# Unread products in the four message passes of a graph and expert network, and another split of the PSUM banks

## The reference, cut to what matters

```
def _gine(x, src, dst, edge_attr, W1, b1, W2, b2, eW, eb, eps):
    e = edge_attr @ eW + eb                                # 31875 x 32 @ 32 x 256
    m = jax.nn.relu(x[src] + e)                            # a gather of 31875 rows of 256
    agg = jax.ops.segment_sum(m, dst, num_segments=N)      # the message pass
    h = (1.0 + eps) * x + agg
    return jax.nn.relu(h @ W1 + b1) @ W2 + b2
h = _gine(x, ...)                                          # pass 1 of 4
for k in range(1, 4):
    y = relu(layernorm(h, gamma[k], beta[k]))
    h = h + _gine(y, ...)                                  # passes 2 to 4
```

## Time and profile before

| | us |
|---|---|
| median of 3 runs | 4527.91 |
| the profiled execution | 4526.65 |
| its span | 4525.0 |
| first to last line 957 in pass 1 | 145 to 549 |
| in pass 2 | 632 to 1023 |
| in pass 3 | 1105 to 1496 |
| in pass 4 | 1576 to 1968 |

### The profile page before, as it was taken

One profiled execution on the slowest core, in us unless ns is written; L12 is line 12 of the kernel. 1 busy time (PEld: TensorE's weight loads), 2 busy tenths in 40 slices (PEclk: granted clock), 3 DMA queues, 4 the chain that ended last, 5 costly groups with the idle time before them and its releaser, 6 DMA issues. The chain is left out here.

```text
span 4525.0 us, 52039 instructions
## 1 busy us (share of the span) xinstructions
PE 2865.0 (63%) x16062; PEld 2374.0 (52%) x16063; DVE 2207.9 (49%) x4940; ACT 726.2 (16%) x1635; POOL 1870.5 (41%) x1982
## 2 busy tenths in 40 slices
PE   3566657775777667750568256767769639947492
PEld 2456545563565455540557123336758639936391
DVE  7566645554555545566246556771254421144213
ACT  1122112221222212210112000002210113300120
POOL 4566456664666366636315666711100020020212
PEclk8788877877777777875769566667979869968696
DMA  5733223332333233313423133317756459945693
GB/s 129 287 87 88 68 67 90 90 84 59 88 89 90 53 90 89 90 34 130 161 54 109 41 92 93 94 43 254 245 185 234 157 183 327 309 149 171 210 338 119
DMA packets 358089, 607.55 MB, mean 134 GB/s; under 512 B 82185, under 2 KB 240187, under 8 KB 355131
## 3 DMA queue, kind: packets, MB, share of 16 engines
q1 hardware_dynamic: 245816, 357.76, 24.3%
q0 software_dynamic: 88640, 214.25, 17.0%
q10 hardware_dynamic: 23363, 32.26, 2.0%
HBM read 508.28 MB, written 95.81 MB: 134 GB/s over the span
## 5 line engine op out<-in xcount | busy, mean ns | idle before, releaser
L831 POOL DMA_INDIRECT gine_got<-gine_table,src x1056 | 1017.4, 963 | 561.2 <-issue 271.4
L905 PE MATMUL gine_p_sum<-gine_hot,gine_got 128*128 128x128 f32 x4224 | 782.9, 330 | 204.5 <-issue 174.0
L905 PEld LDWEIGHTS gine_p_sum<-gine_hot,gine_got 128*128 128x128 f32 x4224 | 690.2, 240 | 289.8 <-issue 266.0
L957 DVE TENSOR_TENSOR gine_got<-gine_got,gine_p_edge 128x512 f32<-128x512 f32 x528 | 360.5, 683 | 601.5 <-DMA unpack_rows<-in_edge_rows 250.7
L916 ACT ACTIVATE gine_got<-gine_got 128x512 f32<-128x512 f32 x528 | 332.2, 630 | 1309.5 <-DVE gine_got L957 946.9
L940 DVE TENSOR_TENSOR stack_acc<-stack_acc,gine_p_sum 128x256 f32 x1056 | 437.6, 414 | 43.0 <-issue 1.5
L489 POOL DMA_INDIRECT adjacency<-value,place x264 | 280.3, 1062 | 390.3 <-POOLq L54 191.4
L892 PE MATMUL gine_p_edge<-gine_w_a,edge_space 128*128 128x256 bf16 x1056 | 329.1, 326 | 98.7 <-issue 94.1
L893 PE MATMUL gine_p_edge<-gine_w_b,edge_space 128*128 128x256 bf16 x1056 | 328.7, 325 | 98.9 <-issue 85.8
L1416 PE MATMUL ffn_p_h<-ffn_xt,ffn_w 128*128 128x128 f32 x2864 | 347.7, 280 | 1.7 <-DVE ffn_xt L1468 0.5
L1416 PEld LDWEIGHTS ffn_p_h<-ffn_xt,ffn_w 128*128 128x128 f32 x2864 | 337.5, 196 | 4.6 <-issue 2.5
(11 more groups left out here) (399 smaller groups left out, 3365.4 us busy)
## 6 DMA issues: line engine op xcount, KB each, us to landing
gcn_a<-adjacency SPq DMA_DIRECT2D x270, 320.0 KB
ffn_w<-in_L_ffn_W SPq DMA_DIRECT2D x74, 1024.0 KB
ffn_w<-in_L_ffn_w SPq DMA_DIRECT2D x60, 1024.0 KB
ffn_w<-in_L_ffn_w SPq DMA_DIRECT2D x90, 512.0 KB
adjacency<-zero_row ACTq DMA_DIRECT2D x3, 7200.0 KB
gine_got<-gine_table,src POOLq DMA_INDIRECT x1056
h_table<-score_rows SPq DMA_DIRECT2D x15, 1056.0 KB
edge_space<-dst_lines ACTq DMA_DIRECT2D x3, 2816.0 KB
```

The lines of the kernel that those rows point to most:

```text
L831: pool.indirect_dma_start(got[:, c % RING, :], None, table, bass.IndirectOffsetOnAxis(ap=rows[:, c:c + 1], axis=0)).then_inc(gathered[c % ...
L905: ins = nc.tensor.matmul(p_sum[q % NB][:, k * D + half * P:k * D + (half + 1) * P], got[:, d % RING, half * P:(half + 1) * P], hot[:, d % ...
L957: nc.vector.tensor_tensor(both, both, p_edge[p % NB][:, :], ALU.add).then_inc(summed, 1)
```

## The change

Three things are edited, all in `gine_edges`. The banks: three of `p_edge` (NE) and four of `p_sum` (NB) in passes 2 to 4, with AHEAD = 2; two of `p_edge` and three of `p_sum` in pass 1, with AHEAD = 2 as before. The bank that this frees becomes `p_spare`. And TensorE gets two more matmuls per couple, one behind the edge products and one behind the sums: float32, 384 columns, the identity as weights against the first two tiles of the node features `g.X`, into `p_spare`. Nothing reads `p_spare`, nothing waits for these products, and they wait for nothing. The second of them is issued only while there are edge products left (and none before the first sums), so a pass has 132 + 130 of them.

```
-        NB = 3 if with_pairs else 4
-        AHEAD = NB - 1
-        p_edge = [ph.ps(f"p_edge{b}", [P, 512]) for b in range(NB)]
+        NE, NB, AHEAD = (2, 3, 2) if with_pairs else (3, 4, 2)
+        p_edge = [ph.ps(f"p_edge{b}", [P, 512]) for b in range(NE)]
         p_sum = [ph.ps(f"p_sum{b}", [P, 512]) for b in range(NB)]
+        p_spare = ph.ps("p_spare", [P, 512])
+        spare = g.X[:, 0:2, :].rearrange("p t d -> p (t d)")
...
-                    if p >= NB:
-                        pe.wait_ge(summed, p - NB + 1)
+                    if p >= NE:
+                        pe.wait_ge(summed, p - NE + 1)
...
                     ins.then_inc(edge_done, 1)
+                    nc.tensor.matmul(p_spare[:, 0:384], g.ident[:, :], spare[:, 0:384], start=True, stop=True)
                 if p >= AHEAD:
...
                     ins.then_inc(agg_done, 1)
+                    if p < EC // 2:
+                        nc.tensor.matmul(p_spare[:, 0:384], g.ident[:, :], spare[:, 0:384], start=True, stop=True)
...
-                    nc.vector.tensor_tensor(both, both, p_edge[p % NB][:, :], ALU.add).then_inc(summed, 1)
+                    nc.vector.tensor_tensor(both, both, p_edge[p % NE][:, :], ALU.add).then_inc(summed, 1)
```

More of the change, by code:

```diff
@@ L886, in _ @@
                 if p < EC // 2:
-                    if p >= NB:
-                        pe.wait_ge(summed, p - NB + 1)
+                    if p >= NE:
+                        pe.wait_ge(summed, p - NE + 1)
                     for k in range(2):
-                        edges = p_edge[p % NB][:, k * D:(k + 1) * D]
+                        edges = p_edge[p % NE][:, k * D:(k + 1) * D]
                         nc.tensor.matmul(edges, g.attrs_t[:, 2 * p + k, :], w_a[:, :], start=True, stop=False)
```

## The result

The changed kernel takes 4564.62 us (median of 4, 4563.25 to 4565.95) against 4526.74 us for the kernel before on the same chip (4 runs, 4521.24 to 4534.96): ratio 1.009, 95% interval 1.0073 to 1.0107. The forecast was 4452 us and faster; it is 38 us slower. On what I call a slow chip (that of this comparison, whose number is not on record, and chip 0 of the experiments) the kernel before takes 4527 us; on chips 1, 10 and 11, the fast ones, 4187 to 4188 us. The changed kernel loses on both: 38 us on the slow one, 102 us on a fast one.

The account below looks back on a forecast made before the run. The prediction took the passes to be bound by TensorE, its own work and stalls, not the gathers. Terms of -87 (passes 2 to 4), +7 (pass 1) and +5 (starts) gave -75 us: 4452 us, range 4380 to 4620.

Parts of the forecast that it names:

- I take 2.75: the wide products break the bursts up: Passes 2 to 4: a couple falls from 2.97 to 2.75 us as stalls after dense narrow bursts shrink, -87 us.
- floor of 2.63: TensorE's work per couple in passes 2 to 4 at 2.4 GHz without waiting: 1.33 + 1.30 us; pass 1, 2.87.
- The evidence called nearer: Stage at 2400 us: wide float32 products busy 41.8 of 50 us beside indirect DMAs, clock 0.95, without falling back.
- The passes are therefore bound by TensorE: All four passes: TensorE's own work and stalls, not the gathers, set today's 2.97 and 2.95 us per couple.
- +5 for the starts: Start of each pass: at most one new product exposed, +5 us for four passes, between 0 and +10.
- 3.00 taken: Pass 1: a couple goes from 2.95 to 3.00 us, +7 us; at the floor of 2.87, -10.
- Banks and AHEAD at nothing: All passes: the shorter bank rings cost nothing; AHEAD = 2 takes at most 2 us off a pass's end, counted 0.
- 0.7 us steps gone: Sign of being right: TensorE no longer starts instructions only every 0.7 us, its "issue" gaps in the passes.
- Edge product to addition under 1 us: Sign of being right, in the passes: VectorE's addition follows TensorE's edge product within 1 us, where 6.4 was read.
- A: Passes: stalls keep their present worth, turn about 2.97 in passes 2 to 4, 3.15 in pass 1; 4515 to 4560 us; 0.09.
- B: Passes: late results stay and add to the longer work; 4627 us with 2 us stalls, 4870 with 5; chance 0.24.
- C: Passes: the clock does not stay up; 3.33 us a couple, 3.28 in pass 1, +185, 4710 us; chance 0.09.

Follow-up runs that it names:

- fill_plain: The changed kernel with its gathers replaced by as many ordinary DMAs of the same size from SP's queue, on a slow chip: 4375.2 us.
- fill_decoupled: The changed kernel with its gathers sent to a separate twelve-slot ring that nobody reads, on a slow chip: 5667.79 us.
- two_edge_banks: The changed kernel without the unread products and with two edge banks instead of three in passes 2 to 4, slow chip: 4527.48 us, ratio 1.0003.
- fill_512: The changed kernel with both unread products widened from 384 to 512 columns, on a slow chip: 4654.54 us, ratio 1.0277.
- fill_thirds: The changed kernel with each unread product made as three of 128 columns, on a fast chip: 4316.08 us, repeated 4315.02 us.
- pause_third: The kernel before with two awaited GpSimd memsets ahead of every third couple's gathers, on a fast chip: 4315.27 us, repeated 4312.49 us.
- after_again: The changed kernel itself, unedited, timed on a fast chip: 4290.12 us, ratio 1.0247 to the kernel before.
- decoupled: The kernel before with its gathers sent to a separate twelve-slot ring that nobody reads, on a fast chip: 4212.7 us, repeated 4212.93 us.

## Why the prediction was wrong

**The step that failed** is "I take 2.75: the wide products break the bursts up", -87 us for passes 2 to 4. Measured are 2.97 to 2.98, so 0 instead of -87. With a floor of 2.63 the 2.75 leaves 0.12 us a couple for stalls; measured are 0.35, one stop of 1.06 us in three couples. The floor itself was right. What was wrong is the cause behind the 2.75, that stalls follow dense bursts of narrow products and that wide ones break them up. On the same kind of chip, with the same products, the stalls are gone when the gathers are replaced by ordinary DMAs (fill_plain, 2.622), and TensorE all but stands still when the gathers run without pause (fill_decoupled, one instruction per 1.40 us). They go with the stream of indirect DMAs, which the change left as it was. The evidence called nearer, has 29 indirect DMAs in 50 us, one in 1.7 us, and not the passes' row of six or eight without a pause.

**Is it TensorE or the gathers?** "The passes are therefore bound by TensorE: by its own work and by these stalls, not by the gathers" holds for the changed kernel on the slow chip: TensorE waits for no engine, and GpSimd and VectorE wait for it. It doesn't hold on a fast chip, where the gathers' 2.51 us is the whole pace before the change, with a TensorE that works for 1.33 us of it. For the kernel before on the slow chip, the waits say TensorE and its stops again (the gathers are 22 us ahead of their additions), but its own work is only 1.33 us a couple at the upper clock. There it is the stops that matter, and the products shortened work that had room beside them.

**Why the pace came out the same.** The slow chip's numbers, from the stops of pass 2 (medians):

```
                    gathers     stop: start     records     pace: per couple
                    per stop    to start, us    per stop    us
before              8           2.86            100         2.95
two_edge_banks      8           2.88            100         2.93
after               6           2.67             99         2.97
```

For the changed kernel TensorE's side adds up: 3 x 2.622 + 1.06 = 8.93 us for three couples. GpSimd's side does too, since it stops with TensorE: of 2.67 us, 1.25 are a gather and 1.42 standing still, and 3 x 2.51 + 1.42 = 8.95. In the kernel before a stop has 1.61 us of standing still for four couples. So on GpSimd's side each stop became cheaper, by 0.19 us, and there are a third more of them: a couple has 33 records of TensorE instead of 25, and a stop comes after about 100 in all three kernels. The results come less late, too: a stopped gather starts 6.0 us (median) after the last matmul of the sums that it waits for, 8.1 before, and 0.55 us is what a gather needs in fill_512. That the two paces agree within 0.02 us is not derived from anything here.

**Theory S is argued, not shown.** For it: the 100 records, and that the first eight stops behind 800 us in the changed kernel all end 1.12 to 1.46 us after the end of the last gather's record, when GpSimd has stopped issuing. Against it: 3 x 33 and 4 x 25 are near 100 also because a cycle is a whole number of couples. In the kernel before TensorE goes on in 0.7 us steps beside the gathers instead of waiting for their pause. And in fill_decoupled it crawls for 28 to 31 us after GpSimd has stopped for good. The two kernels that would have tested S (fill_thirds, pause_third) never met a slow chip. Another possibility stands untested: every execution on record has a span and a granted clock of its own, taken by the profiler, so no run tells whether the recording of TensorE's instructions has a part in its stops.

The Trainium skill, "Runtime: NRT & Kernel Launch", section "Instruction fetch mechanics", says that an engine's instructions come by DMA in blocks of 16 KiB, 256 instructions, and that the cost of this is mostly hidden. The first half agrees with after_again, where packets of 16,384 bytes of the kind instruction are 20.3 us apart on average (633.18 to 714.36), 256 records at 33 per 2.62 us. But a stop every 100 records isn't that block, and in fill_decoupled such a packet (945.85 us) came before the crawl; whether it was TensorE's the trace doesn't say. Where instructions wait between block and engine no run here shows.

**Where the 38 us are.** From first edge addition to last gather pass 2 takes 381.2 us instead of 376.5 (640.8 to 1022.0, 631.6 to 1008.1); from there to the last addition into `acc` 23.9 instead of 20.1, since what is left in the ring is worked off at TensorE's own price, which the products have doubled. Pass 1: +0.8 and +6.1 us. With 3 x (4.7 + 3.8) that is 32 of the spans' 36.6 us. The prediction had +5 for the starts and 0 for the ends ("takes at most 2 us off a pass's end").

**Point by point.** TensorE's work: 2.63 and 2.87 worked out, 2.622 and 2.91 measured on a fast chip (and 2.622 in fill_plain on a slow one). The price of a product, 0.65 us: 128 more columns of 384 in both raised the pace by 0.43 (3.05 less 2.62), as 0.65/3 x 2 says. Pass 1: 3.00 taken, 3.00 measured, by luck: it had been 3.01 by the same reading, not 2.95, and of the 3.00 TensorE's work is 2.91 (fill_plain) and the rest stops. Banks and AHEAD at nothing: right, 1.0003 and 0.999. Clock above 0.95: right, and worth nothing. 0.7 us steps gone: no, but fewer, 33 to 41 a pass in passes 2 to 4 where there were 118 to 131 (starts of loads and matmuls 0.65 to 0.75 us apart). Edge product to addition under 1 us: no, 4.3 us in the median, 6.8 before, 0.31 in fill_512, and 6.7 on a fast chip without any stop. Line 957 every 2.7 to 2.8: no. The 130.0 us in which GpSimd is said to stand idle "beside its own 0.30 us gaps" contain these gaps, 77 us of them: the stops are 53.

**The rivals.** A came true in passes 2 to 4 in its number ("the turn is again about 2.97"); it had 0.09, and its band of 4515 to 4560 ended 5 us under the result. (Its lower end, -12 us, doesn't follow from its terms: a turn of 2.90 is -28 us, and pass 1 +26.) B, "Late results stay and add to the longer work", came true in its mechanism: three couples are 3 x 2.62 us of work and one stop. It had 0.24, and its rule that "the change loses as soon as more than 1.4 us of stall per four couples is left" fits to the tenth: 1.06 us in three couples are 1.4 in four, and the passes neither win nor lose. Its two stalls, 2 us for +100 and 5 us for +345, were too long. (With 5 us, four couples are 15.5 us and 3.88 a couple, not 15 and 3.75.) C failed: the clock stays up. The section of the Trainium skill cited for C, "A second HAM failure mode: psum-queue depth-cycling" in "TensorE: Matmul & The Clock Gate", is borne out by no run: fast-chip passes that cycle the same banks without products hold 0.94 to 1.00. On the slow chip the low clock goes with TensorE standing still: 0.50, the lower level, all through fill_decoupled's crawl.

On a fast chip the prediction's own numbers give the right answer: a pace bound by gathers at 2.5 and a new floor of 2.63 and 2.87 is a loss. The low clock was read as a part of the cause; in the changed kernel it is gone, and the pace of 2.97 is still there.

## What to carry over

Before filling an engine with work that nobody reads, to raise its clock, show that its own work is what ends last: here it was 1.33 of 2.5 us, and the fill made a free engine the bound. If a pace stays above every engine's floor, ask which engine's activity the late ones go with; one kernel in which that activity is replaced or decoupled from its readers answers it in a single run, if it meets the chip that has the trouble. Don't take the distance from a result to its use for lateness before you know how old the other input is. And compare on more than one chip: the same kernel differed by 8% between two, and the change by 0.9% and 2.5%.

## What the hardware showed

- Chips differ where indirect DMAs run. The kernel before takes 4527 us on chip 0 and 4187 to 4188 on chips 1, 10 and 11; 254 of the 339 us are in the passes. fill_plain, whose passes are equal to after_again's, keeps the other 85 (4375.2 against 4290.1). Of these 81 arise between 2192 and 2759 us of after_again, where half of the 264 indirect DMAs into `adjacency` and all 264 from `h_table` are issued; the rest of the program differs by 4 us. On any one chip the times of the kernel before lie within 0.5% of each other, but each chip save chip 10 was met in one batch of runs: that it is the chip, and not the hour, is the likely reading and not shown.
- On chip 0 a stream of back-to-back indirect DMAs (1.30 us apart) leaves TensorE one instruction per 1.40 us, for over 300 us and for 28 to 31 us after its end, after some 13 us at full speed; VectorE's additions stay at 0.69 us (fill_decoupled). On chips 10 and 11 such a stream changes nothing for the kernel without the products (decoupled, 1.77 us a couple as without gathers).
- With a pause after every second gather (1.25 and 1.80 us by turns, fill_512, pass 2) TensorE has no stops, at nearly the same mean distance (1.52 us) as in the changed kernel (1.49), which has one in three couples. More work on TensorE can hide the stops so, at a price above its worth.
- On a fast chip the clock is at 0.97 in a stretch in which matmuls are busy for 209 of 328 us; on the slow one at 0.78 with 277 of 391.
